# First-attention products issued one block later in a fused attention and quantised-layer kernel

## The chip, the cores and the metric

The kernel runs on one core of a Trainium2 chip. One launch computes all 16 images. The metric is the device time of that launch in microseconds. Six things work side by side on the core: TensorE (PE in the profile; its weight loads are PEld), VectorE (DVE), ScalarE (ACT), GpSimd (POOL), SyncE (SP, which here only issues transfers) and the DMA engines. Each engine runs its own list of instructions strictly in order and waits at semaphores for the others, so an instruction that waits holds everything behind it on its engine.

## The reference, cut to what matters

For each image, with x of 256 channels by 1024 places (tokens):

```python
def reference(x, norm_w, norm_b, qkv_w, qkv_b, proj_w, proj_b, ffn_w, ffn_b):
    xn = group_norm(x, norm_w, norm_b)                   # 8 groups
    q, k, v = split(einsum('oc,bchw->bohw', qkv_w, xn) + qkv_b)
    attn = softmax(einsum('bci,bcj->bij', q, k) / sqrt(C))
    x = x + (einsum('oc,bchw->bohw', proj_w, einsum('bij,bcj->bci', attn, v)) + proj_b)
    t = to_tokens(x)
    y = layer_norm(t)
    yn = y / (norm(y) + 1e-12)
    s = einsum('bid,bjd->bij', yn, yn)
    t = t + einsum('bij,bjd->bid', softmax(s * s), y)    # second attention
    z = layer_norm(t) @ (sign(w - mean(w)) * mean(abs(w))) + ffn_b
    t = t + round(clip(z, -1, 1) * 7) / 7
    return from_tokens(t)
```

## The kernel before

**Tiling.** The 1024 tokens are 8 blocks of 128. A 1024x1024 score matrix is made block by block: one block is 128 rows by 1024 columns. Every fp32 operand is kept as two rounded parts, a high one (`_hi`) and the rest (`_lo`), and each product is three matmuls (lo by hi, hi by lo, hi by hi).

**First attention, per block n.** TensorE makes `scores1(n)` in `wide[n % 2]` (L369). VectorE takes the row maximum, `row_max` (L989). ScalarE takes the exponential, `exp1` (L733). The block is then needed transposed. VectorE transposes inside 32x32 squares, `e1_turn` (L996); SyncE sends it to a scratch in HBM, `send` (L321), and fetches it back in the other order as four transfers, `fetch` (L328). ScalarE rounds it, `e1T_hi` (L740), VectorE takes the rest, `e1T_lo` (L1001), and only then can TensorE run `product1(n)` (L471 to L473, 24 matmuls). A product follows its block's scores by several blocks, to cover this round trip. `residual1(n)` on VectorE (L1010 to L1017) adds the input and takes the layer norm's statistics.

**After it.** For small groups of blocks (`GROUPS1`: two, two, two, one, one) GpSimd works out the layer norm's coefficients and lengths (L1250 to L1273), ScalarE makes `layer_norm1` (L750, L754) and `unit_rows` (L762), TensorE transposes these (`turn_cos`, L500), ScalarE and VectorE split them (`cosT_hi` L774, `cosT_lo` L1023). `scores2` (L369) makes the lower triangle of the symmetric second scores, `exp2` (L787, L789) their exponentials, and `turn_e2` (L530), `e2T_parts` (L1040, L1042) the upper triangle. `product2` follows in `back`.

**Between batches.** The older image `f = b - 1` runs its last layer inside `front(b, f)`: `turn_ln2`, `ffn`, and two output turns, `turn_t(f, 0)` and `turn_t(f, 1)` (L577), whose results VectorE adds in `output` (L1079). The next image's group norm statistics (`gn_sums` L952, L954) are taken on VectorE in the same stretch, and two tiny matmuls average them over groups, `group_means` (L411) and `group_vars` (L416).

**What sets the order.** The order of each engine's calls is written out by hand in the five functions `front`, one for each engine. There is no scheduler and no priority. The loop runs over images 1 to 14; image 0 and image 15 are written out with the same functions.

**Semaphores that matter below.** `scores1(n)` waits for `exp1(n - 2)`, since they share `wide[n % 2]`. `product1(n)` waits for `e1T_lo(n)`. `fetch(n)` waits for `send(n)` to have landed and for `e1T_lo(n - 2)`. `e1T_hi(n)` waits for `fetch(n)` and `product1(n - 2)`. `product1(4)` uses the bank that `output(f, 1)` must have read. `scores2(0)` waits for `cosT_lo(0)`. `scores2(4)` waits for `cosT_lo(2)`.

Of the kernel before, what the change touches and what calls it, by code (L numbers as in the profile page):

```python
# [45 lines left out]
def build(nc, x, norm_w, norm_b, qkv_w, qkv_b, proj_w, proj_b, ffn_w, ffn_b, out):  # L46
# [22 lines left out]
    with ExitStack() as ctx:  # L69
# [223 lines left out]
        def _(sp):  # L293
# [36 lines left out]
            def front(b, f):  # L330
# [8 lines left out]
                fetch(b, 3)  # L339
                fetch(b, 4)  # L340
                send(b, 5)
                fetch(b, 5)
                send(b, 6)
                fetch(b, 6)
                send(b, 7)
# [18 lines left out]
        def _(pe):  # L364
# [216 lines left out]
            def front(b, f, more):  # L581
# [37 lines left out]
                if f is not None:  # L619
                    pe.wait_ge(y_made, 4 * f + 4)  # L620
                    turn_t(f, 0)
                product1(b, 0)
                scores1(b, 5)
# [3 lines left out]
                product1(b, 1)  # L627
                scores1(b, 6)
                product1(b, 2)
                scores1(b, 7)  # L630
                turn_cos(b, 0)
                product1(b, 3)
# [7 lines left out]
                product1(b, 5)  # L640
                product1(b, 6)
                turn_cos(b, 1)
                turn_e2(b, 1)
                product1(b, 7)
                scores2(b, 2)
                turn_cos(b, 2)
                scores2(b, 3)
                turn_e2(b, 2)
                if more:
                    pe.wait_ge(t1_made, NT * b + 6)  # L650
                    group_means(b + 1)
# [3 lines left out]
                if more:  # L655
                    group_vars(b + 1)
# [3 lines left out]
                scores2(b, 6)  # L660
                turn_e2(b, 5)
# [42 lines left out]
        def _(act):  # L704
# [100 lines left out]
            def front(b, f, more, reuse=True):  # L805
# [20 lines left out]
                exp1(b, 4)  # L826
                e1T_hi(b, 2)
                exp1(b, 5)
                e1T_hi(b, 3)
                layer_norm1(b, 0)  # L830
                exp1(b, 6)
                unit_rows(b, 0)
                e1T_hi(b, 4)
                cosT_hi(b, 0)
                exp1(b, 7)
                e1T_hi(b, 5)
                e1T_hi(b, 6)
                exp2(b, 0)
                exp2(b, 1)
                layer_norm1(b, 1)  # L840
                unit_rows(b, 1)
                e1T_hi(b, 7)
                layer_norm1(b, 2)
                cosT_hi(b, 1)
                unit_rows(b, 2)
                layer_norm1(b, 3)
                exp2(b, 2)
                cosT_hi(b, 2)
# [3 lines left out]
                unit_rows(b, 4)  # L852
                cosT_hi(b, 3)
                exp2(b, 4)
                cosT_hi(b, 4)
# [42 lines left out]
        def _(dve):  # L898
# [183 lines left out]
            def front(b, f, more):  # L1082
# [29 lines left out]
                row_max(b, 4)  # L1112
                if f is not None:
                    output(f, 0)
                e1_turn(b, 4)
                e1T_lo(b, 1)
                residual1(b, 0)
                row_max(b, 5)
                e1T_lo(b, 2)
                e1_turn(b, 5)  # L1120
                residual1(b, 1)
                if f is not None:
                    output(f, 1)
                row_max(b, 6)
# [250 lines left out]
```

## Time and profile before

| | us |
|---|---|
| median of 3 runs | 1841.47 |
| lowest, highest | 1837.36, 1841.86 |
| the profiled execution | 1838.67 |
| its span in the profile | 1836.7 |
| TensorE busy | 1761.3 (96%) |
| VectorE busy | 1330.1 (72%) |
| ScalarE busy | 945.8 (51%) |
| GpSimd busy | 735.2 (40%) |
| HBM traffic | 92 GB/s over the span |

TensorE's busy time is a union of overlapping matmuls, so a busy TensorE still may be slowed by its clock. The idle time of the other engines costs nothing by itself. What counts are the places where TensorE waits, and these repeat nearly alike in each image. All rows from one image below are from batch 5, whose first attention runs around 600 to 645 us of the span.

### The profile page before, as it was taken

Reading aid. Unit: us, or ns where it says so; the run is one execution under the profiler, and the core shown is the slowest. Engines: PE = TensorE matmul, PEld = TensorE weight load, DVE = VectorE, ACT = ScalarE, POOL = GpSimd, SP = SyncE. Lnnn points to the kernel's source line nnn. Section 1 sums busy time; section 2 is a strip of 40 time slices with the busy share of each in tenths; the row PEclk is TensorE's granted clock in tenths of the full one; section 3 lists DMA queues with packets and bytes.
Section 4 is the critical chain, followed back from the end, with each engine's and each line's share of the span. In section 5 each row is a group of like instructions: output and inputs, shape, how many; then the busy total and the mean of one; then the engine's idle time right before and its main releaser. Section 6 shows DMA issues by size and latency. Waiting matters only on the chain.

```text
span 1836.7 us, 34581 instructions
## 1 busy us (share of the span) xinstructions
PE 1761.3 (96%) x11810; PEld 1610.9 (88%) x11810; DVE 1330.1 (72%) x2596; ACT 945.8 (51%) x1476; POOL 735.2 (40%) x1334
## 2 busy tenths in 40 slices
PE   8999999999999999999999999999999999999997
PEld 6898888988889888898988989888898888998887
DVE  6767767687676877768777686776868768686675
ACT  3645546455464554635456354564545545455462
POOL 0442615327162361624516245261542715326161
PEclk9999999999999999999999999999999999999998
DMA  3405124050330604216042150412405134050330
GB/s 122 140 24 155 52 95 133 23 174 32 118 111 33 193 2 133 96 40 189 0 148 80 57 171 14 158 57 74 154 23 164 42 99 129 23 178 28 95 113 24
DMA packets 108575, 169.67 MB, mean 92 GB/s; under 512 B 12928, under 2 KB 79872, under 8 KB 108544
## 3 DMA queue, kind: packets, MB, share of 16 engines
q1 hardware_dynamic: 108544, 169.27, 29.0%
q8 instruction: 18, 0.29, 0.1%
q14 instruction: 13, 0.11, 0.0%
HBM read 85.33 MB, written 83.89 MB: 92 GB/s over the span
## 4 chain that ended last, share of the span: by engine, by line
PE 55%; issue 19%; POOL 11%; DVE 8%; ACT 4%; DMA 1%; SPq 0%; POOLq 0%; DVEq 0%; ACTq 0%
PE wide L369 21%; PE narrow L369 5%; PE narrow L471 4%; PE narrow L473 4%; PE wide L471 4%; PE narrow L472 3%; PE wide L473 3%; PE wide L472 3%; PE turn L530 2%; DVE gn_stats L952 2%; POOL ln_r L1253 2%; PE turn L424 2%; PE turn L569 2%; PE turn L560 1%; POOL ln_shift L1255 1%
## 5 line engine op out<-in xcount | busy, mean ns | idle before, releaser
L369 PE MATMUL wide<-xn_hi,prob 128*128 128x512 f32 x1024 | 303.8, 398 | 0.3 <-ACT expo L733 0.3
L1250 POOL TENSOR_TENSOR ln_v<-ln_mv,ln_eps 128x2 f32<-128x2 f32 (+2 forms) x128 | 34.1, 266 | 542.3 <-DVE ln_mv L1017 332.9
L369 PEld LDWEIGHTS wide<-xn_hi,prob 128*128 128x128 f32 x1024 | 185.5, 188 | 39.2 <-ACT expo L733 0.7
L740 ACT ACTIVATE prob<-e_back 128x1024 fp32r<-128x1024 f32 x128 | 135.4, 1058 | 149.2 <-DMA e_back<-e_scratch 134.7
L767 ACT ACTIVATE ln<-tok,ln_shift,ln_r 128x256 f32<-128x256 f32 x128 | 68.5, 593 | 263.9 <-POOL ln_shift L1255 263.9
L996 DVE STREAM_TRANSPOSE x_norm<-expo 128x1024 f32<-128x1024 f32 x128 | 159.1, 1243 | 48.3 <-ACT expo L733 41.6
L733 ACT ACTIVATE expo<-wide,neg_max 128x1024 f32<-128x1024 f32 x128 | 142.3, 1111 | 98.9 <-DVE neg_max L989 98.9
L1001 DVE TENSOR_TENSOR prob<-e_back,prob 128x1024 fp32r<-128x1024 f32 x128 | 155.5, 1214 | 45.6 <-ACT prob L740 44.8
L989 DVE TENSOR_REDUCE neg_max<-wide 128x1 f32<-128x1024 f32 x128 | 155.2, 1212 | 41.4 <-PE wide L369 41.4
L1295 POOL TENSOR_TENSOR carrier_p<-ones 128x1 f32<-128x1 f32 x60 | 11.7, 195 | 415.4 <-DVE y_sb L1065 412.8
L369 PE MATMUL wide<-xn_lo,prob 128*128 128x512 f32 x512 | 160.7, 394 | 0.0
L1285 POOL TENSOR_TENSOR prob<-expo,prob 128x128 fp32r<-128x128 f32 (+6 forms) x112 | 143.1, 1290 | 36.8 <-DVE prob L1029 36.8
L471 PE MATMUL narrow<-prob 128*128 128x256 f32 x512 | 147.7, 288 | 1.9 <-DVE prob L1001 1.9
L471 PE MATMUL wide<-val,prob 128*128 128x258 f32 x512 | 147.1, 287 | 0.0
L471 PE MATMUL narrow<-val,prob 128*128 128x258 f32 x512 | 146.9, 287 | 0.0
L473 PE MATMUL narrow<-prob 128*128 128x256 f32 x512 | 145.4, 284 | 0.0
L472 PE MATMUL narrow<-prob 128*128 128x256 f32 x512 | 145.3, 284 | 0.0
L473 PE MATMUL wide<-val,prob 128*128 128x258 f32 x512 | 145.1, 283 | 0.0
L473 PE MATMUL narrow<-val,prob 128*128 128x258 f32 x512 | 145.1, 283 | 0.0
L472 PE MATMUL wide<-val,prob 128*128 128x256 f32 x512 | 144.6, 282 | 0.0
L472 PE MATMUL narrow<-val,prob 128*128 128x256 f32 x512 | 144.6, 282 | 0.0
L471 PE MATMUL wide<-prob 128*128 128x256 f32 x384 | 114.4, 298 | 23.4 <-DVE prob L1001 23.4
(182 smaller groups left out, 5466.8 us busy)
## 6 DMA issues: line engine op xcount, KB each, us to landing
e_scratch<-x_norm SPq DMA_DIRECT2D x128, 512.0 KB, 3.0
e_back<-e_scratch SPq DMA_DIRECT2D x512, 128.0 KB, 3.1
x_raw<-in_x SPq DMA_DIRECT2D x32, 512.0 KB, 4.0
out<-y_sb SPq DMA_DIRECT2D x32, 512.0 KB, 3.7
tok<-in_L_conv_qkv_w SPq DMA_DIRECT2D x1, 768.0 KB, 6.6
ln<-in_L_conv_proj_w SPq DMA_DIRECT2D x1, 256.0 KB, 6.8
ln<-in_L_ffn_weight SPq DMA_DIRECT2D x1, 256.0 KB, 3.9
out_bias<-in_L_conv_proj_b SPq DMA_DIRECT2D x1, 128.0 KB, 3.8
```

The costliest lines, as they stand in the source:

```text
L369: mm = pe.matmul(o, lhsT, r, start=first and i == 0, stop=last and i == len(parts) - 1)
L424: mm = pe.transpose(turn[:, t * C + k * P:t * C + (k + 1) * P], x_raw[:, k, tile(HT * g + t)], ident[:, :])
L471: pe.matmul(o[:, 0:w], hi, value_hi(j), start=j == 0, stop=False)
L472: pe.matmul(o[:, 0:C], hi, value_lo(j), start=False, stop=False, skip_group_check=True)
L473: mm = pe.matmul(o[:, 0:w], lo, value_hi(j), start=False, stop=j == NT - 1)
L733: act.activation(expo[:, n % DEEP], wide[n % 2][:, :], ACT.Exp, bias=neg_max[:, n:n + 1], accum_out=row_sum1[:, n:n + 1]).then_inc(e1_made, 1)
L740: act.activation(eT_hi[:, n % 2].rearrange("p (n i t) -> p n i t", n=NT, i=SQ), e_back[:, n % 2].rearrange("p i (n t) -> p n i t", n=NT), ...
L767: act.activation(ln2[:, n], tok[:, n], ACT.Identity, bias=ln2_shift[:, n:n + 1], scale=ln2_r[:, n:n + 1]).then_inc(ln2_made, 1)
L989: dve.tensor_reduce(neg_max[:, n:n + 1], wide[n % 2][:, :], AX.X, ALU.max, negate=True).then_inc(max_made, 1)
L996: dve.transpose(e_turned[:, n % 2].rearrange("p (q n t) -> p n q t", q=SQ, n=NT), expo[:, n % DEEP].rearrange("p (n q t) -> p n q t", q=SQ ...
L1001: dve.tensor_sub(eT_lo[:, n % 2].rearrange("p (n i t) -> p n i t", n=NT, i=SQ), e_back[:, n % 2].rearrange("p i (n t) -> p n i t", n=NT), ...
L1285: pool.tensor_sub(prob[:, 1, J, row], expo[:, J % DEEP, row], prob[:, 0, J, row].bitcast(F32)).then_inc(p_made, 1)
```

## The change

The calls in the five hand-written orders are moved; none is added or taken away, and no line of a called function changes.

- TensorE: `scores1(5)`, `scores1(6)` and `scores1(7)` each stand one place earlier against the products. `turn_t(f, 1)` stands after `scores1(7)` and no longer before `product1(1)`. `turn_cos(1)` and `turn_cos(2)` stand earlier, `group_means` and `group_vars` later.
- ScalarE: `exp1(5)`, `exp1(6)`, `exp1(7)` come earlier against the rounding `e1T_hi`; `layer_norm1(0)` comes after `exp1(7)`.
- VectorE: the row maxima, turns, rests and residuals are reordered to match. `output(f, 1)` comes after `row_max(7)`. `gn_sums(b + 1, 1)`, `gn_deviation` and `gn_variance` come later.
- SyncE: `send(5)`, `send(6)` and `send(7)` each stand one place ahead of a `fetch`.
- GpSimd's order is the same.

```diff
--- before.py
+++ after.py
@@ -337,12 +337,12 @@
                 fetch(b, 2)
                 send(b, 4)
                 fetch(b, 3)
+                send(b, 5)
                 fetch(b, 4)
-                send(b, 5)
+                send(b, 6)
                 fetch(b, 5)
-                send(b, 6)
+                send(b, 7)
                 fetch(b, 6)
-                send(b, 7)
                 fetch(b, 7)
                 if f is not None:
                     store(f, 0)
@@ -619,17 +619,17 @@
                 if f is not None:
                     pe.wait_ge(y_made, 4 * f + 4)
                     turn_t(f, 0)
+                scores1(b, 5)
                 product1(b, 0)
-                scores1(b, 5)
+                scores1(b, 6)
+                product1(b, 1)
+                scores1(b, 7)
                 if f is not None:
                     pe.wait_ge(out_made, 2 * f + 1)
                     turn_t(f, 1)
-                product1(b, 1)
-                scores1(b, 6)
                 product1(b, 2)
-                scores1(b, 7)
+                product1(b, 3)
                 turn_cos(b, 0)
-                product1(b, 3)
                 if f is not None:
                     pe.wait_ge(out_made, 2 * f + 2)
                 else:
@@ -638,26 +638,26 @@
                 scores2(b, 0)
                 scores2(b, 1)
                 product1(b, 5)
+                turn_cos(b, 1)
                 product1(b, 6)
-                turn_cos(b, 1)
                 turn_e2(b, 1)
                 product1(b, 7)
+                turn_cos(b, 2)
                 scores2(b, 2)
-                turn_cos(b, 2)
                 scores2(b, 3)
                 turn_e2(b, 2)
-                if more:
-                    pe.wait_ge(t1_made, NT * b + 6)
-                    group_means(b + 1)
                 scores2(b, 4)
                 turn_cos(b, 3)
                 turn_e2(b, 3)
                 if more:
-                    group_vars(b + 1)
+                    pe.wait_ge(t1_made, NT * b + 6)
+                    group_means(b + 1)
                 scores2(b, 5)
                 turn_e2(b, 4)
                 turn_cos(b, 4)
                 scores2(b, 6)
+                if more:
+                    group_vars(b + 1)
                 turn_e2(b, 5)
                 scores2(b, 7)
                 scores2(b, 8)
@@ -824,34 +824,34 @@
                     ffn_out(f, 1, reuse)
                 e1T_hi(b, 1)
                 exp1(b, 4)
+                exp1(b, 5)
                 e1T_hi(b, 2)
-                exp1(b, 5)
+                exp1(b, 6)
                 e1T_hi(b, 3)
+                exp1(b, 7)
                 layer_norm1(b, 0)
-                exp1(b, 6)
+                e1T_hi(b, 4)
                 unit_rows(b, 0)
-                e1T_hi(b, 4)
+                e1T_hi(b, 5)
                 cosT_hi(b, 0)
-                exp1(b, 7)
-                e1T_hi(b, 5)
+                layer_norm1(b, 1)
                 e1T_hi(b, 6)
+                unit_rows(b, 1)
                 exp2(b, 0)
                 exp2(b, 1)
-                layer_norm1(b, 1)
-                unit_rows(b, 1)
+                cosT_hi(b, 1)
                 e1T_hi(b, 7)
                 layer_norm1(b, 2)
-                cosT_hi(b, 1)
                 unit_rows(b, 2)
                 layer_norm1(b, 3)
+                cosT_hi(b, 2)
                 exp2(b, 2)
-                cosT_hi(b, 2)
                 unit_rows(b, 3)
                 exp2(b, 3)
                 layer_norm1(b, 4)
-                unit_rows(b, 4)
                 cosT_hi(b, 3)
                 exp2(b, 4)
+                unit_rows(b, 4)
                 cosT_hi(b, 4)
                 exp2(b, 5)
                 exp2(b, 6)
@@ -1110,55 +1110,55 @@
                 if f is not None:
                     clip(f, 1)
                 row_max(b, 4)
+                e1T_lo(b, 1)
+                e1_turn(b, 4)
                 if f is not None:
                     output(f, 0)
-                e1_turn(b, 4)
-                e1T_lo(b, 1)
+                row_max(b, 5)
+                e1_turn(b, 5)
                 residual1(b, 0)
-                row_max(b, 5)
+                row_max(b, 6)
                 e1T_lo(b, 2)
-                e1_turn(b, 5)
+                e1_turn(b, 6)
                 residual1(b, 1)
+                e1T_lo(b, 3)
+                row_max(b, 7)
                 if f is not None:
                     output(f, 1)
-                row_max(b, 6)
-                e1T_lo(b, 3)
-                e1_turn(b, 6)
-                row_max(b, 7)
+                e1_turn(b, 7)
+                residual1(b, 2)
                 e1T_lo(b, 4)
-                e1_turn(b, 7)
+                residual1(b, 3)
+                e1T_lo(b, 5)
                 cosT_lo(b, 0)
-                e1T_lo(b, 5)
-                residual1(b, 2)
-                residual1(b, 3)
+                residual1(b, 4)
                 e1T_lo(b, 6)
-                residual1(b, 4)
                 e2_hi(b, 0)
                 e2_hi(b, 1)
                 residual1(b, 5)
+                cosT_lo(b, 1)
                 e1T_lo(b, 7)
                 residual1(b, 6)
-                cosT_lo(b, 1)
+                e2T_parts(b, 1)
                 if more:
                     gn_sums(b + 1, 0)
-                e2T_parts(b, 1)
                 residual1(b, 7)
+                cosT_lo(b, 2)
+                e2_hi(b, 2)
+                e2T_parts(b, 2)
+                e2_hi(b, 3)
                 if more:
                     gn_sums(b + 1, 1)
-                e2_hi(b, 2)
-                cosT_lo(b, 2)
-                e2T_parts(b, 2)
-                if more:
-                    gn_deviation(b + 1)
-                e2_hi(b, 3)
                 cosT_lo(b, 3)
                 e2T_parts(b, 3)
                 if more:
-                    gn_variance(b + 1)
+                    gn_deviation(b + 1)
                 e2_hi(b, 4)
                 e2T_parts(b, 4)
                 cosT_lo(b, 4)
                 e2_hi(b, 5)
+                if more:
+                    gn_variance(b + 1)
                 e2T_parts(b, 5)
                 e2_hi(b, 6)
                 e2_hi(b, 7)
```

On ScalarE, in the loop's `front`, this stands before, from `exp1(6)` (its source is `wide0`) over `unit_rows(0)`, `e1T_hi(4)`, `cosT_hi(0)` and `exp1(7)` (`wide1`) to `e1T_hi(5)` and `e1T_hi(6)`:

```order
L733 ACTIVATE expo,row_sum1<-wide0,neg_max 128x1024
L758 REGISTER_ALU
L762 ACTIVATE cos_x<-ln_x,len_i 128x256 x2
L737 REGISTER_ALU
L740 ACTIVATE prob<-e_back 128x1024
L774 ACTIVATE tokT_hi<-narrow1 128x2x256
L730 REGISTER_ALU
L733 ACTIVATE expo,row_sum1<-wide1,neg_max 128x1024
L740 ACTIVATE prob<-e_back 128x1024
L737 REGISTER_ALU
L740 ACTIVATE prob<-e_back 128x1024
```

and now, from `exp1(6)` over `e1T_hi(3)`, `exp1(7)`, `layer_norm1(0)` (L750, L754), `e1T_hi(4)` and `unit_rows(0)` to `e1T_hi(5)`:

```order
L733 ACTIVATE expo,row_sum1<-wide0,neg_max 128x1024
L740 ACTIVATE prob<-e_back 128x1024
L730 REGISTER_ALU
L733 ACTIVATE expo,row_sum1<-wide1,neg_max 128x1024
L746 ISA
L750 ACTIVATE ln_x<-tok,ln_shift,ln_r 128x256 x2
L754 ACTIVATE val<-ln_x 128x2x256
L737 REGISTER_ALU
L740 ACTIVATE prob<-e_back 128x1024
L758 REGISTER_ALU
L762 ACTIVATE cos_x<-ln_x,len_i 128x256 x2
L740 ACTIVATE prob<-e_back 128x1024
```

The first layer norm, the rounding of block 4 and the first unit rows stood ahead of block 7's exponential and stand behind it now.

On VectorE, at the last row maximum (its source is `wide1`), this stands before, from `output(f, 1)` over `row_max(6)`, `e1T_lo(3)`, `e1_turn(6)`, `row_max(7)`, `e1T_lo(4)` and `e1_turn(7)` to `cosT_lo(0)`:

```order
L1079 TENSOR_TENSOR y_sb<-turn,y_sb 128x1024
L988 REGISTER_ALU
L989 TENSOR_REDUCE neg_max<-wide0 128x1
L1001 TENSOR_TENSOR prob<-e_back,prob 128x1024
L995 REGISTER_ALU
L996 STREAM_TRANSPOSE x_norm<-expo 128x8x4x32
L988 REGISTER_ALU
L989 TENSOR_REDUCE neg_max<-wide1 128x1
L1001 TENSOR_TENSOR prob<-e_back,prob 128x1024
L996 STREAM_TRANSPOSE x_norm<-expo 128x8x4x32
L1022 ISA
L1023 TENSOR_TENSOR tokT_lo<-narrow1,tokT_hi 128x2x256
```

and now, from `e1T_lo(3)` over `row_max(7)`, `output(f, 1)`, `e1_turn(7)` and `residual1(2)` to `e1T_lo(4)`:

```order
L1001 TENSOR_TENSOR prob<-e_back,prob 128x1024
L988 REGISTER_ALU
L989 TENSOR_REDUCE neg_max<-wide1 128x1
L1079 TENSOR_TENSOR y_sb<-turn,y_sb 128x1024
L996 STREAM_TRANSPOSE x_norm<-expo 128x8x4x32
L1010 RECIPROCAL inv_sum1<-row_sum1 128x1
L1012 SCALAR_TENSOR_TENSOR tok<-narrow0,inv_sum1,x_tok 128x256
L1015 BN_STATS ln_stats<-tok 128x6
L902 MEMSET carrier 128x1
L1017 BN_AGGR ln_mv<-ln_stats 128x2
L1001 TENSOR_TENSOR prob<-e_back,prob 128x1024
```

The output of the older image moved behind the last row maximum, and the rest of block 4 moved behind the last turn and a residual.

On VectorE, after `residual1(7)`, this stands before, from `gn_sums(b + 1, 1)` to `cosT_lo(2)`:

```order
L952 BN_STATS gn_stats<-x_raw 128x6 x2
L901 REGISTER_ALU
L902 MEMSET carrier 128x1
L954 BN_AGGR gn_mv<-gn_stats 128x2
L1028 REGISTER_ALU
L1029 CAST prob<-expo 128x384
L1022 REGISTER_ALU
L1023 TENSOR_TENSOR tokT_lo<-narrow1,tokT_hi 128x2x256
```

and now, from `cosT_lo(2)` over `e2_hi(2)`, `e2T_parts(2)` and `e2_hi(3)` to the same group norm sums:

```order
L1023 TENSOR_TENSOR tokT_lo<-narrow1,tokT_hi 128x2x256
L1028 REGISTER_ALU
L1029 CAST prob<-expo 128x384
L1039 REGISTER_ALU
L1040 CAST prob<-turn 128x2x128
L1042 TENSOR_TENSOR prob<-turn,prob 128x2x128
L1028 REGISTER_ALU
L1029 CAST prob<-expo 128x512
L952 BN_STATS gn_stats<-x_raw 128x6 x2
L901 REGISTER_ALU
L902 MEMSET carrier 128x1
L954 BN_AGGR gn_mv<-gn_stats 128x2
```

The sums moved from ahead of `cosT_lo(2)` to behind block 3's copy.

## Rows read from the trace of the kernel before

**Rows 1.** Waits of TensorE: engine, line, releaser: us in total, times, longest

```profile
PE wide L471 <- DVE prob L1001: 23.4, 16, 1.7
PE narrow L411 <- DVE gn_mv L954: 15.8, 13, 7.3
PE narrow L500 <- ACT cos_x L762: 11.5, 16, 0.9
PE wide L369 <- DVE tokT_lo L1023: 7.7, 16, 0.6
```

**Rows 2.** TensorE in order of time, batch 5: start us, duration us, engine, line, operation

```profile
610.00 1.06 PE L577 MATMUL turn<-ident,tok 128*128 128x128 f32 x8
...
613.77 0.64 PE L369 MATMUL wide<-xn_hi,prob 128*128 128x512 f32 x2
...
616.57 1.03 PE L577 MATMUL turn<-ident,tok 128*128 128x128 f32 x8
```

**Rows 3.** TensorE, the same view, later in batch 5; idle time before a row in brackets

```profile
632.10 0.28 PE L471 MATMUL turn<-prob 128*128 128x256 f32 x1
...
634.98 0.22 PE L369 MATMUL wide<-tokT_hi,tokT_lo 128*128 128x128 f32 x1
...
636.37 0.28 PE L471 MATMUL narrow<-prob 128*128 128x256 f32 x1
...
643.06 0.63 PE L500 MATMUL narrow<-ident,cos_x 128*128 128x128 f32 x4 [0.78 <-ACT cos_x L762]
...
645.25 0.39 PE L471 MATMUL wide<-prob 128*128 128x256 f32 x1 [1.45 <-DVE prob L1001]
...
653.81 0.56 PE L369 MATMUL wide<-tokT_hi,tokT_lo 128*128 128x384 f32 x2 [0.48 <-DVE tokT_lo L1023]
...
656.37 0.59 PE L369 MATMUL wide<-tokT_hi,tokT_lo 128*128 128x512 f32 x2
```

**Rows 4.** VectorE in order of time, same batch

```profile
610.56 1.22 DVE L989 TENSOR_REDUCE neg_max<-wide 128x1 f32<-128x1024 f32 x1
...
616.52 0.15 DVE L1010 RECIPROCAL inv_sum<-row_sum 128x1 f32<-128x1 f32 x1
...
617.79 1.23 DVE L989 TENSOR_REDUCE neg_max<-wide 128x1 f32<-128x1024 f32 x1
...
629.00 1.22 DVE L989 TENSOR_REDUCE neg_max<-wide 128x1 f32<-128x1024 f32 x1 [0.60 <-PE wide L369]
...
643.97 1.23 DVE L1001 TENSOR_TENSOR prob<-e_back,prob 128x1024 fp32r<-128x1024 f32 x1 [2.59 <-ACT prob L740]
```

**Rows 5.** ScalarE in order of time, same batch

```profile
611.97 1.06 ACT L740 ACTIVATE prob<-e_back 128x1024 fp32r<-128x1024 f32 x1 [2.05 <-DMA e_back<-e_scratch]
...
624.17 1.10 ACT L750 ACTIVATE ln_x<-tok,ln_shift,ln_r 128x256 f32<-128x256 f32 x2 [1.43 <-POOL ln_shift L1255]
...
625.84 1.10 ACT L733 ACTIVATE expo<-wide,neg_max 128x1024 f32<-128x1024 f32 x1
...
628.12 1.04 ACT L740 ACTIVATE prob<-e_back 128x1024 fp32r<-128x1024 f32 x1
```

**Rows 6.** GpSimd in order of time, same batch

```profile
637.36 1.17 POOL L1250 TENSOR_TENSOR ln_v<-ln_mv,ln_eps 128x2 f32<-128x2 f32 x1 [8.91 <-DVE ln_mv L1017]
```

**Rows 7.** SyncE queue in order of time, same batch

```profile
637.15 1.73 SPq L328 DMA_DIRECT2D e_back<-e_scratch  x4
```

**Rows 8.** DMA issues: bytes of one, median us from issue to landing

```profile
e_back<-e_scratch SPq DMA_DIRECT2D x512, 128.0 KB, 3.1
```

**Rows 9.** Two neighbouring batches: us, TensorE busy (instructions), granted clock, DMA share, GB/s

```profile
529.55:643.06 113.51, 109.81 (x736) 0.98 0.28 92
643.06:754.95 111.89, 108.25 (x737) 1.00 0.29 93
```

**Rows 10.** 3.4 us before and after a fall of the granted clock, same columns

```profile
536.20:539.60 3.40, 2.40 (x14) 1.00 0.00 0
539.60:543.00 3.40, 2.91 (x13) 0.66 0.00 0
```

## The prediction

> **What bounds the kernel now.** I read the share of busy time first, then the waits of TensorE, then one batch in order of time on every engine. TensorE is busy for 96% of the span, so the change can only touch its waits and its clock. Four waits matter [rows 1]: the first attention's last product waits for its rest (23.4 us over 16 batches), `group_means` waits for the group sums (15.8, of which 7.3 are one wait at the start), `turn_cos(1)` waits for the unit rows (11.5), and `scores2(4)` waits for `cosT_lo(2)` (7.7). Without the 7.3 that is 51 us, 3.2 in a batch. These waits stand late in the first attention and after it: 0.78 us ahead of 643.06, 1.45 ahead of 645.25, 0.48 ahead of 653.81 [rows 3]. No product before the last one waits for its rest. The reader is to see that the other engines bound the tail of a stage whose body TensorE bounds.
>
> A second cost is TensorE's clock. Neighbouring batches take 113.51 and 111.89 us, with a mean granted clock of 0.98 and 1.00 [rows 9]. In the slower one the clock fell from 2.4 to 1.2 GHz for some 3 us, right behind the stretch with the short waits: 2.40 of 3.40 us busy ahead, then a mean clock of 0.66 [rows 10]. One fall costs about 1.6 us, and one batch in two has it.
>
> **TensorE's side of the change.** An output turn and the product behind it take 613.77 - 610.00 = 3.77 us together, a score block 616.57 - 613.77 = 2.80 [rows 2], a product alone 634.98 - 632.10 = 2.88 [rows 3]; so the turn is some 0.8, its product starting a little slower. I follow batch 5. Everything up to the output turn at 610.00 is unchanged. The new order gives `scores1(5)` 610.8 to 613.6, `product1(0)` to 616.5, `scores1(6)` to 619.3, `product1(1)` to 622.2, `scores1(7)` to 625.0. One output turn and one product have moved from ahead of the last score block to behind it, so it ends 3.8 us earlier than the 628.8 that the old order gives (616.57 + 0.8 + 2.9 + 2.8 + 2.9 + 2.8). TensorE does the same work, so this is worth nothing unless the last product's rest comes as much earlier.
>
> **VectorE's side.** Its large instructions let the next one start after 1.14 us (a duration of 1.22 less an overlap of 0.08), a residual after 617.79 - 616.52 = 1.27 [rows 4]. ScalarE's exponential takes 1.2 us with its sum. From `row_max(4)` at 610.56 the new order is:
> - `e1T_lo(1)` has to wait for its rounding, which ends at 611.97 + 1.06 = 613.03 [rows 5]. The old order had `output(f, 0)` in this hole. So `e1T_lo(1)` 613.1, `e1_turn(4)` 614.3, `output(f, 0)` 615.4, `row_max(5)` 616.6 to 617.8. The old order had it at 617.79 [rows 4].
> - `exp1(5)` to 619.0, `e1_turn(5)` 619.1, `residual1(0)` 620.2, `row_max(6)` 621.5, `e1T_lo(2)` 622.7, `e1_turn(6)` 624.0, `residual1(1)` 625.2, `e1T_lo(3)` 626.5, `row_max(7)` 627.6.
>
> The old order had `row_max(7)` at 629.00 [rows 4]. So of the 3.8 us only 1.4 arrive: VectorE's queue is the limit, not the scores.
>
> **ScalarE's side, where the change costs.** `exp1(7)` runs 628.9 to 630.0. `layer_norm1(0)` stands behind it, although its coefficients are there by then; its three instructions take 625.84 - 624.17 = 1.67 us [rows 5]. `e1T_hi(4)` comes next, 631.7 to 632.7, where the old order had it at 628.12 [rows 5], ahead of `exp1(7)`. Then `e1T_lo(4)` ends at 634.0 and `product1(4)` starts at 634.05. The old start was 632.10 [rows 3]. TensorE meanwhile has done `turn_t(f, 1)`, `product1(2)` and `product1(3)` by 625.0 + 0.8 + 2.9 + 2.9 = 631.6. **A new wait of 2.1 us** stands here, part of it written down to `turn_cos(0)`, whose unit rows come at 633.5.
>
> **What it gives back.** `product1(4)` to 637.0, two small score blocks 636.37 - 634.98 = 1.4 [rows 3] to 638.4, `product1(5)` to 641.3. The statistics of `residual1(3)` are there at 635.3. In the old trace GpSimd started on that group at 637.36 and the turn on TensorE at 643.06, 5.7 us later [rows 3, 6]; this now gives 641.0, so the wait of 0.8 ahead of `turn_cos(1)` goes. `product1(6)` runs 641.8 to 644.7. `e1T_hi(7)` stands behind the two first `exp2` and `cosT_hi(1)` and ends at 643.9. VectorE has `residual1(5)` and `cosT_lo(1)` ahead of `e1T_lo(7)`, which then runs 644.6 to 645.8 (old: 643.97 [rows 4]). The last product starts at 645.85, against 645.25 [rows 3]. Its wait shrinks from 1.45 to about 1.0.
>
> **Behind it.** `turn_cos(2)` now stands right behind the last product, and its unit rows are some 0.3 us late. `turn_e2(2)` waits for `exp2(2)`, some 0.6 us, as ScalarE has `layer_norm1(3)` ahead. The wait of 0.48 ahead of `scores2(4)` goes, since the group sums no longer stand ahead of `cosT_lo(2)`. They stand behind the copy of block 3 now and end at 656.3, so `group_means` waits 0.7 us as before. `scores2(5)` starts at 656.5, against 656.37 [rows 3], and `group_vars` (0.14 us) no longer is ahead of it. **Sum: 0.3 us a batch more, 5 us in 16 batches.** Later steps (`product2`, the older image's layer) have the same order and start from there; image 0 has no older image and is counted like the rest.
>
> **Transfers.** `fetch(4)` now waits for `e1T_lo(2)`, which ends at 623.9. Landing takes 1.73 of issue and up to 3.1 more [rows 7, 8], so 628.7 at the latest; `e1T_hi(4)` takes it at 631.7. Cover 3 us. `fetch(7)` follows `e1T_lo(5)`, 636.5, lands by 641.3, and is taken at 642.8. Cover 1.5 us. The sends gain a place and lose nothing. I take 0 for all of these; if the covers went, each us late is paid once.
>
> **How far off the sum can be.** The step with the widest play is GpSimd's first instruction of a group. Started during a VectorE instruction with two inputs in SBUF, it took 1.17 us [rows 6], and I assumed that again; without it `e1T_lo(6)`, the last product and the second coefficient chain come up to 0.9 earlier, of which TensorE could use some 0.5. The other end is two such hits more, and the slower first matmul after each wait, together 0.8 a batch. So the sum lies between -0.2 and +1.1 us a batch, -3 to +18 in all. I take +0.3, since the rows that it hangs on show the hit.
>
> **The clock.** Nothing in the trace says when it will fall with the waits elsewhere. The bounds are no fall (8 x 1.6 = 13 us gained) and one in each batch (13 lost). I take a fall or two less, -2 us, as the longest single stretch of waits before (0.78 and 1.45 close together) is broken up. The Trainium skill, "TensorE: Matmul & The Clock Gate", section "Why this matters for your kernels", warns only of idle gaps longer than any that stand here. By that rule the clock would have stayed up, and the new wait would cost no more than its length, 1841.5 + 5 = 1846.5. The trace disagrees already: the clock fell behind waits of at most 1.45 us [rows 3, 10].
>
> **Rivals.**
> - **A, balance (0.41).** As worked out: +5 for the waits and -2 for the clock, so 1838.7 + 3 = 1841.7 for the profiled execution. The median of three stands 2.8 us over that execution, so 1844.5. Its own range is 1837 to 1847.
> - **B, faster (0.24).** The last product's rest comes early enough, because GpSimd is not held up, and the falls of the clock behind it go. -3 for the waits and -8 for five falls less: 1841.5 - 11 = 1830.5. For it: the old waits stand exactly where the clock fell. Against: VectorE hands on only 1.4 of the 3.8 us.
> - **C, slower (0.24).** The new wait of 2.1 us ahead of `product1(4)` is the longest of all. If the clock falls behind it in each batch, 8 falls come on top: 1841.5 + 5 + 13 = 1859.5. It decides once the wait there is about as long as the two old ones together (2.2 us, and 2.1 is forecast); `layer_norm1(0)` behind `exp1(7)` is its cause. Against: the old pair of waits brought a fall in one batch of two only.
> - **D, slower by the later chain (0.11).** Coefficients of the third and fourth group, each late by the hit on GpSimd: 0.8 a batch more than A, 1841.5 + 13 + 3 = 1857.
>
> That the change does not do what it says is no rival here: the order is what is written, and no planner stands between.
>
> **How the numbers follow.** The forecast is A, 1844.5 us. B lies below the bound of 0.3% (5.5 us, about what a measurement of this kernel can tell from no change), C and D above it. So faster 0.24, same 0.41, slower 0.35. The range that leaves out two in ten, one at each end, is 1830 to 1860; it takes in -3 to +18 for the waits.
>
> **What would show it.** In the new profile: TensorE waits about 2 us ahead of `product1(4)` (line L471 into `turn`) or `turn_cos(0)`, in each batch; the wait ahead of the last product is near 1.0; the one of `scores2(4)` for `cosT_lo` is gone, that of `group_means` stays. `row_max(7)` comes about 17.0 us after `row_max(4)`. If the wait ahead of `product1(4)` is under 1 us, the reading of ScalarE's queue is wrong and B is right. If the waits sum as said and the time does not, it is the clock.

## The result and the profile after

The changed kernel takes 1835.8 us (median of 20), the kernel before 1840.2 us (median of 20). The ratio is 0.9978, with a 95% interval of 0.9970 to 0.9985. That is 0.22% faster: inside the band of 0.3% that the prediction called the same, but clear of zero and on the other side of the forecast, which stood 0.16% above the median of before that it knew. The profiled execution takes 1835.49 us.

The span and the first part of the page of the changed kernel, beside the table of before:

```profile
span 1833.8 us, 34581 instructions
...
PE 1753.4 (96%) x11810; PEld 1603.2 (87%) x11810; DVE 1370.1 (75%) x2596; ACT 930.8 (51%) x1476; POOL 726.8 (40%) x1334
```

TensorE's waits in the changed kernel (same columns as [rows 1]):

```profile
PE narrow L500 <- ACT cos_x L762: 32.8, 32, 2.3
PE narrow L411 <- DVE gn_mv L954: 17.9, 16, 7.3
PE turn L530 <- ACT expo L789: 10.1, 16, 0.7
PE wide L471 <- DVE prob L1001: 6.0, 9, 0.7
```

Two of the four of before have shrunk or gone: the last product waited 23.4 us in all and waits 6.0, and `scores2(4)` no longer waits for `cosT_lo(2)`. New is a wait for the unit rows ahead of `turn_cos(0)` (nearly all of the 32.8), and the one for `exp2(2)` has grown to 10.1. Without the one at the start (7.3) the four add up to 59.5 us, against 51 of the four in [rows 1]. The wait for `exp2(2)` was 3.3 us before and is not in that 51:

```profile
PE turn L530 <- ACT expo L789: 3.3, 12, 0.3
```

So some 5 us of waits have come. **By its waits the kernel should be slower.**

Batch 5 on TensorE, the places of [rows 3]. The first output turn, at 610.00 in before, starts at 608.96 here, so 1.04 us is to be added to these times to set them beside the prediction's:

```profile
632.64 0.63 PE L500 MATMUL narrow<-ident,cos_x 128*128 128x128 f32 x4 [1.84 <-ACT cos_x L762]
633.15 0.39 PE L471 MATMUL turn<-prob 128*128 128x256 f32 x1
...
644.76 0.39 PE L471 MATMUL wide<-prob 128*128 128x256 f32 x1 [0.68 <-DVE prob L1001]
...
648.09 0.63 PE L500 MATMUL narrow<-ident,cos_x 128*128 128x128 f32 x4 [0.20 <-ACT cos_x L762]
...
651.78 0.44 PE L530 MATMUL turn<-ident,expo 128*128 128x128 f32 x2 [0.63 <-ACT expo L789]
...
655.23 0.38 PE L411 MATMUL narrow<-gn_mv,group_mean 128*128 128x2 f32 x2 [0.70 <-DVE gn_mv L954]
655.48 0.59 PE L369 MATMUL wide<-tokT_hi,tokT_lo 128*128 128x512 f32 x2
```

VectorE (`row_max(4)`, `row_max(7)`, `e1T_lo(4)`, `cosT_lo(2)`) and ScalarE (`exp1(7)`, `layer_norm1(0)` in two rows, `e1T_hi(4)`), the places of [rows 4] and [rows 5]:

```profile
609.51 1.22 DVE L989 TENSOR_REDUCE neg_max<-wide 128x1 f32<-128x1024 f32 x1
...
626.64 1.22 DVE L989 TENSOR_REDUCE neg_max<-wide 128x1 f32<-128x1024 f32 x1
...
631.80 1.30 DVE L1001 TENSOR_TENSOR prob<-e_back,prob 128x1024 fp32r<-128x1024 f32 x1 [0.17 <-ACT prob L740]
...
650.83 0.69 DVE L1023 TENSOR_TENSOR tokT_lo<-narrow,tokT_hi 128x512 fp32r<-128x512 f32 x1 [1.54 <-ACT tokT_hi L774]
```

```profile
627.90 1.11 ACT L733 ACTIVATE expo<-wide,neg_max 128x1024 f32<-128x1024 f32 x1 [3.95 <-DVE neg_max L989]
...
629.00 1.08 ACT L750 ACTIVATE ln_x<-tok,ln_shift,ln_r 128x256 f32<-128x256 f32 x2
630.12 0.63 ACT L754 ACTIVATE val<-ln_x 128x512 fp32r<-128x512 f32 x1
630.66 1.04 ACT L740 ACTIVATE prob<-e_back 128x1024 fp32r<-128x1024 f32 x1
```

GpSimd, the first coefficient instruction of the second group, as in [rows 6]:

```profile
634.45 1.09 POOL L1250 TENSOR_TENSOR ln_v<-ln_mv,ln_eps 128x2 f32<-128x2 f32 x1 [2.43 <-DVE ln_mv L1017]
```

Two neighbouring batches (columns of [rows 9]), from one start of `turn_cos(0)` to the next:

```profile
519.74:632.64 112.90, 109.54 (x737) 0.98 0.29 93
632.64:744.98 112.34, 108.30 (x736) 1.00 0.30 93
```

And the wait of `turn_cos(0)` with what follows it, in a batch with a fall of the clock and in the next one; then the wait alone and the time behind it alone, in the batch with the fall:

```profile
517.90:521.30 3.40, 1.56 (x8) 0.79 0.39 157
630.80:634.20 3.40, 1.56 (x12) 1.00 0.38 154
```

```profile
517.90:519.70 1.80, 0.00 (x0) 1.00 0.71 291
519.90:522.90 3.00, 3.00 (x16) 0.50 0.43 129
```

An undisturbed batch takes 112.34 us, 0.45 more than the 111.89 of before. A batch with a fall takes 112.90, where before it took 113.51 [rows 9]. Before, this fall cost 1.6 us; here it costs 0.56. The clock falls at 519.87, right behind the wait, while `turn_cos(0)` runs. Its slow product 4 makes TensorE busy for 1.24 us more (109.54 against 108.30) and eats the wait that the last product would have had (0.68 in an undisturbed batch, none in the other).

The clock record of the two traces has 14 falls before and 9 after; without the two at the very end, in both, 12 and 7. **What a fall costs depends on the waits that follow it:**

| falls in the trace | right behind | batch with one | costs |
|---|---|---|---|
| before, batches 1, 4, 6, 8, 10, 12, 14 | the waits of `turn_e2(2)`, `group_means`, `scores2(4)` (0.3, 0.7, 0.5) | 113.29 to 113.57 | 1.6 |
| before, batches 2 and 13 | the wait of the last product (1.45) | 111.90 and 111.88 | 0 |
| changed, batches 2, 4, 6, 8, 9, 11, 13 | the wait of `turn_cos(0)` (1.84) | 112.84 to 112.93 | 0.56 |

The other three of before lie in batch 0 (two) and in batch 15. The batch that costs nothing, in before:

```profile
1544.50:1656.38 111.88, 109.22 (x736) 0.98 0.29 93
```

TensorE is busy for 0.98 us more there (109.22 against 108.25), and the waits of `turn_e2(2)` and `group_means` behind the fall, 0.98 us together, are gone. So in batches 1 to 14 the change did not lower the number of falls that cost something, seven and seven, but their price.

In the profiled pair the thirteen batches from the second on take the same time, 112.64 us each (before, then changed):

```profile
192.07:1656.38 1464.31, 1418.58 (x9568) 0.99 0.29 93
182.03:1646.45 1464.42, 1416.66 (x9569) 0.99 0.30 93
```

A longer undisturbed batch and cheaper falls cancel there. By the starts of `turn_cos(4)` the changed kernel is 1.9 us ahead in batch 1 and still 1.9 us ahead in batch 14. The rest of the 2.9 us between the two spans comes behind it.

### The profile page after: what moved, and what is told of

Read it like the earlier page. It is cut to its first block, busy times and chain, and to the rows that moved or that the text cites. A ratio compares the mean times of both kernels' runs of the same rounds, so it can differ in the third digit from the quotient of the medians.

```text
span 1833.8 us, 34581 instructions
## 1 busy us (share of the span) xinstructions
PE 1753.4 (96%) x11810; PEld 1603.2 (87%) x11810; DVE 1370.1 (75%) x2596; ACT 930.8 (51%) x1476; POOL 726.8 (40%) x1334
## 4 chain that ended last, share of the span: by engine, by line
PE 52%; issue 19%; POOL 15%; ACT 6%; DVE 6%; DMA 1%; POOLq 1%; SPq 0%; ACTq 0%; DVEq 0%
PE wide L369 19%; PE narrow L369 5%; PE narrow L471 4%; PE narrow L473 3%; PE wide L471 3%; PE narrow L472 3%; PE wide L473 3%; PE wide L472 3%; POOL ln_r L1253 2%; PE turn L530 2%; POOL ln_v L1250 2%; POOL val L1279 2%; POOL sq_root L1267 2%; PE turn L424 2%; PE turn L569 2%
## 5 line engine op out<-in xcount | busy, mean ns | idle before, releaser
L1250 POOL TENSOR_TENSOR ln_v<-ln_mv,ln_eps 128x2 f32<-128x2 f32 (+2 forms) x128 | 55.3, 432 | 508.7 <-DVE ln_mv L1017 300.6
L369 PE MATMUL wide<-tokT_hi,tokT_lo 128*128 128x512 f32 (+3 forms) x384 | 122.9, 361 | 0.0
```

The costliest lines, as they stand in the source:

```text
L369: mm = pe.matmul(o, lhsT, r, start=first and i == 0, stop=last and i == len(parts) - 1)
L1250: pool.tensor_add(v[:, cols], mv[:, cols, 1], ln_eps[:, one]).then_inc(steps, 1)
```

## The experiments

Two theories stand. **Clock:** the order itself is slower, as forecast, and the gain is that the falls of the clock cost less. **Waits:** the late waits that went are the gain, and the clock falls as it likes. All times are medians; ratios are to the kernel before, run on the same chip in the same rounds.

### Activity in the waits of the kernel before

```diff
+            def fill(o, count):
+                for _ in range(count):
+                    pe.matmul(o, sign_w[:, 0, 0:P], sign_w[:, 0, :], start=True, stop=True)
...
+                fill(out1[7][:, 0:C], 6)
                 turn_cos(b, 1)
                 turn_e2(b, 1)
+                fill(out1[7][:, 0:C], 11)
                 product1(b, 7)
...
+                    fill(narrow[0][:, 0:C], 5)
                     group_means(b + 1)
...
+                if J == 4:
+                    pe.wait_ge(sq2_made, NP * b + J - 1)
+                    fill(wide[0][:, 0:C], 3)
```

> The kernel before, with 25 extra small matmuls of constants in each batch, into banks that the next instruction overwrites, placed inside TensorE's four waits (6 ahead of turn_cos(1), 11 ahead of the last product, 5 ahead of group_means, 3 ahead of scores2(4); about 0.12 us each). The waits last as long as before, only TensorE is active in them. Clock theory (the gain of the change is fewer falls of the clock, and these follow inactive stretches): the falls go, 12 of them at 1.2 to 1.6 us, so 1840 minus 12 to 18, about 1825 us, and the granted clock is near 1.0 throughout. Rival (the waits themselves are what the change saves, and the clock falls for other reasons): same time as before or slightly more, 1840 to 1844 us, with as many falls.

Measured: 1827.8 us, ratio 0.9930 (0.9916 to 0.9945). Its waits, and one batch:

```profile
PE narrow L411 <- DVE gn_mv L964: 7.3, 1, 7.3
PE turn L537 <- ACT expo L799: 4.2, 15, 0.4
```

```profile
539.66:651.56 111.90, 111.32 (x762) 1.00 0.29 94
```

The waits are now filled, the batch is 111.90 us long as the undisturbed one of before was, and its clock is 1.00. The trace has 3 falls for 14, one in batch 0 and two at the end. More work, 11 us less time: the falls of the clock were caused by TensorE's short inactivity, and they cost the kernel before some 11 us (10.9 by the medians; by the ratio 13, 10 to 15). Seven falls at 1.6 us, as the trace has them, are 11.2.

### The same in the changed kernel

```diff
                     pe.wait_ge(t1_made, NT * b + 2)
+                    fill(narrow[1][:, 0:C], 14)
                 pe.wait_ge(cos_made, NT * b + n1)
```

> The changed kernel, with 14 extra small matmuls of constants in each batch inside the new wait ahead of turn_cos(0), where all seven falls of its clock lie. Clock theory: the falls go, at some 0.6 us each, so 4 us less, about 1832 us. Rival: no change, 1836 us, or more if the extra matmuls delay something.

Measured: 1833.8 us, ratio 0.9966 (0.9953 to 0.9978). Two neighbouring batches are alike now:

```profile
531.39:643.78 112.39, 110.05 (x751) 1.00 0.29 93
```

Only the two falls at the end are left, and 2.0 us are saved; I had expected 4, from 0.6 us each. With the clock out of the way the two orders can be compared: 1833.8 - 1827.8 = **6.0 us slower** for the changed order, 112.39 against 111.90 in a batch. The forecast for the waits was +5. Falls cost 10.9 us in the order before (1838.7 in these rounds less 1827.8) and 2.0 in the changed one (1835.8 less 1833.8), so the clock's part of the change is -8.9. The two parts make -2.9 where the result has -4.3, since the median of the kernel before was 1840.2 in the rounds of the result and 1838.7 in these: the split is good to 1 or 2 us, its signs are not in doubt.

### Work added where TensorE never waits

```diff
                     return prob[:, 0, j, tile(n)], prob[:, 1, j, tile(n)]
 
+                if n == 5:
+                    fill(out2[1][:, 0:C], 4)
```

> The kernel before with 4 extra small matmuls (0.48 us of TensorE work) in each batch ahead of product2(5), where TensorE never waits. Plain sum: 16 batches times 0.48 = 8 us slower, 1848 us. Clock theory: the undisturbed batch grows from 111.9 to 112.4 us, as in the changed kernel, and falls become rarer, one in more than two batches, which gives back most of it: 1840 to 1843 us.

> The kernel before with 8 extra small matmuls (0.96 us) a batch ahead of product2(5). Plain sum: 15 us slower than before, 1855 us. Clock theory: the undisturbed batch is 112.9 us, above the mean of 112.65 at which the falls came out before, so most falls are gone (14 became 13 with half the work added); what is not given back is at most 15 less 12 falls at 1.3, so 1842 to 1848 us.

Measured with 4: 1841.2 us, ratio 1.0007 (0.9997 to 1.0016), so by the ratio 1.3 us (at most 3) for 8 us of added work. With 8: 1842.9 us, ratio 1.0029 (1.0019 to 1.0040), so 5 us for 15. Two batches of the first:

```profile
529.09:641.32 112.23, 108.68 (x740) 1.00 0.29 92
641.32:755.12 113.80, 110.20 (x740) 0.99 0.29 92
```

The added work is there, as the undisturbed batch is 112.23 us and the other 113.80. The falls are 13 with four and 11 with eight extra matmuls, but most of them stand in the place where they are free. One such batch, with a fall behind the last product's wait:

```profile
1206.04:1318.40 112.36, 109.71 (x741) 0.98 0.29 93
```

Of the falls in batches 1 to 14, seven stood in the dear place before, two do with four extra matmuls (batches 5 and 9) and one with eight (batch 1, 113.95 us). At 1.6 us each that gives back 8 and 10 us. The undisturbed batch is longer by 0.42 and by 0.96 us, 7 and 15 us in all. The sums are -1 and +5; the profiled executions stand 0.8 below and 3.5 above the one of before. Why the falls moved is not shown.

### The group part alone, the products' part alone

The first has the kernel before with the later `group_means`, `group_vars`, `gn_sums`, `gn_deviation` and `gn_variance`:

```diff
-                if more:
-                    pe.wait_ge(t1_made, NT * b + 6)
-                    group_means(b + 1)
                 scores2(b, 4)
                 turn_cos(b, 3)
                 turn_e2(b, 3)
                 if more:
-                    group_vars(b + 1)
+                    pe.wait_ge(t1_made, NT * b + 6)
+                    group_means(b + 1)
                 scores2(b, 5)
```

> The kernel before with only the later place of group_means, group_vars and the group sums; products, scores and output turns as before. By the sums of waits: the wait ahead of scores2(4) (0.48) goes, the one ahead of group_means stays near 0.7, so 0.3 to 0.6 us a batch less on an undisturbed batch, 5 to 8 us. Rival, that the clock holds the batch at the same mean: 1838 to 1841 us, the shorter batch paid with more falls.

Measured: 1839.1 us, ratio 0.9995 (0.9986 to 1.0004). The 5 to 8 us that I expected are not there. The time is the rival's, but its reason, a shorter batch paid for with more falls, is not what happened:

```profile
PE wide L471 <- DVE prob L1001: 23.8, 17, 1.7
PE wide L369 <- DVE tokT_lo L1023: 20.0, 16, 1.5
PE narrow L411 <- DVE gn_mv L954: 7.3, 1, 7.3
```

The wait of `group_means` has gone (7.3 is the one at the start), and the one of `scores2(4)` has grown from 7.7 to 20.0, as TensorE gets there earlier and `cosT_lo(2)` does not. The undisturbed batch is longer, some 112.2 us against 111.9, and the falls are fewer, 12 for 14.

The second is the changed kernel with the group part as before:

```diff
                 turn_e2(b, 2)
+                if more:
+                    pe.wait_ge(t1_made, NT * b + 6)
+                    group_means(b + 1)
                 scores2(b, 4)
                 turn_cos(b, 3)
                 turn_e2(b, 3)
                 if more:
-                    pe.wait_ge(t1_made, NT * b + 6)
-                    group_means(b + 1)
+                    group_vars(b + 1)
                 scores2(b, 5)
```

> The changed kernel with group_means, group_vars and the group sums where they stood before; scores, products and output turns as changed. Waits as I read them now: ahead of turn_cos(0) 1.84 us as in the changed kernel; ahead of scores2(4) about 0.5 again, since the sums again stand ahead of cosT_lo(2). So up to 0.5 us a batch above the changed kernel, 8 us. Clock theory: part of that is given back, 1836 to 1842 us. Rival (the later groups are the whole gain): 1840 us or more, with the clock falling as often as before (14 times).

Measured: **1828.6 us**, ratio 0.9937 (0.9925 to 0.9950), 7 us faster than the whole change. My expectation was 1836 to 1842.

```profile
PE narrow L500 <- ACT cos_x L762: 31.8, 32, 1.9
PE turn L530 <- ACT expo L789: 10.0, 16, 0.7
PE narrow L411 <- DVE gn_mv L954: 7.3, 1, 7.3
PE wide L471 <- DVE prob L1001: 4.7, 7, 0.7
```

```profile
519.08:631.25 112.17, 109.54 (x737) 0.98 0.29 94
631.25:742.85 111.60, 108.19 (x736) 1.00 0.30 94
```

The wait of `group_means` has gone and none has come for `cosT_lo(2)`. The profile of the changed kernel has the reason, in its row of VectorE at 650.83: it is idle for 1.54 us ahead of `cosT_lo(2)`, whose rounding is late. In the old place the group sums fill this hole for nothing. In the new place they stand behind block 3's copy and `group_means` waits 0.70 us for them, 15 times. The falls are nearly as many as before (12 for 14) but cheap: 112.17 us against 111.60.

With 14 fills inside the wait of `turn_cos(0)` in this kernel:

> The products-only kernel with 14 extra small matmuls of constants inside the wait of turn_cos(0). All ten of its falls in batches lie in that wait and cost 0.5 us each. Clock theory: no falls in the batches, 1828.6 less 5, about 1823 us; that is 16 times 0.3 us under the filled kernel before (1827.8), the sum of the waits alone. Rival (falls cost nothing here): 1828 us.

Measured: 1821.4 us, ratio 0.9904 (0.9889 to 0.9919). The trace has 3 falls, so nine have gone and with them 7 us, 0.8 each. And the products' part alone is 6.4 us faster than before when neither has falls in its batches (1827.8 - 1821.4), which is 0.4 us a batch. The +6.0 us of the whole change are thus -6.4 for the products and +12.4 (1833.8 - 1821.4) for the later group sums and means on top of them. The falls of this kernel do not lie in the wait, as the expectation has it, but 0.4 to 1.6 us behind its end.

### The queue of ScalarE behind the new wait

```diff
                 exp1(b, 7)
-                layer_norm1(b, 0)
                 e1T_hi(b, 4)
+                layer_norm1(b, 0)
                 unit_rows(b, 0)
...
                 e1_turn(b, 7)
-                residual1(b, 2)
                 e1T_lo(b, 4)
+                residual1(b, 2)
...
                 product1(b, 3)
-                turn_cos(b, 0)
...
                 product1(b, 4)
+                turn_cos(b, 0)
+                product1(b, 5)
                 scores2(b, 0)
                 scores2(b, 1)
-                product1(b, 5)
```

> The changed kernel with three further moves: on ScalarE e1T_hi(4) ahead of layer_norm1(0), on VectorE e1T_lo(4) ahead of residual1(2), on TensorE turn_cos(0) behind product1(4) and the two first blocks of the second scores behind product1(5). If the new wait of 1.84 us is the place of e1T_hi(4) behind the layer norm, as the prediction said, product1(4) starts some 1.6 us later than product1(3) ends no more but about 0.8 us; shorter by 0.3 to 1.0 us a batch, 1820 to 1832 us with the clock's part. Rival (VectorE's or the transfers' pace holds block 4): the wait moves to product1(4) with its old length, 1836 us or more.

Measured: 1827.7 us, ratio 0.9930 (0.9917 to 0.9943). TensorE in batch 5:

```profile
627.99 0.39 PE L471 MATMUL turn<-prob 128*128 128x256 f32 x1 [0.76 <-DVE prob L1001]
...
631.72 0.36 PE L471 MATMUL narrow<-prob 128*128 128x256 f32 x1 [0.16 <-DVE prob L1001]
...
636.39 0.63 PE L500 MATMUL narrow<-ident,cos_x 128*128 128x128 f32 x4 [0.17 <-ACT cos_x L762]
...
640.86 0.39 PE L471 MATMUL wide<-prob 128*128 128x256 f32 x1 [0.79 <-DVE prob L1001]
...
651.33 0.38 PE L411 MATMUL narrow<-gn_mv,group_mean 128*128 128x2 f32 x2 [0.71 <-DVE gn_mv L954]
```

The wait of 1.84 has become 0.76 ahead of `product1(4)`, 0.16 ahead of `product1(5)` and 0.17 ahead of `turn_cos(1)`. That the new wait comes from the place of `e1T_hi(4)` behind the layer norm, as the prediction said, fits this, and the rows of the changed kernel have the chain: `e1T_hi(4)` follows the layer norm at 630.66, VectorE stands idle for it and ends the rest at 633.10, `product1(4)` starts at 633.15. The three moves were measured together only, so their shares are not shown.

No fall is left in the batches, although nothing was filled. With 0.19 ahead of `turn_cos(2)` and 0.63 ahead of `turn_e2(2)` TensorE waits 3.4 us in this batch, and 3.7 in an undisturbed one of before. None of the waits here is above 0.8 us, and they stand over 3 us apart; those of before stood in two groups, two and three of them close together. The sum of the waits alone does not bring the falls.

The other swap was on the kernel before, and took away what ended its longest wait:

```diff
                 layer_norm1(b, 1)
-                unit_rows(b, 1)
                 e1T_hi(b, 7)
+                unit_rows(b, 1)
```

> The kernel before with one swap on ScalarE: e1T_hi(7) ahead of unit_rows(1). If the last product's wait is ScalarE's queue, as the trace has it (the rounding begins at 642.82, the block's data is there near 641.5), the wait of 1.45 us goes down to about 0.3 and the one of turn_cos(1) grows from 0.78 to about 1.2: 1.0 us a batch less, 1823 to 1830 us. Rival by the clock: the shorter batch is paid back with more falls, 1836 to 1840 us.

> The kernel before with that swap and with extra small matmuls of constants inside the waits (9 ahead of turn_cos(1), 3 ahead of the last product, 5 ahead of group_means, 3 ahead of scores2(4)). Clock theory: with no falls left the whole saving of the swap arrives, 1.0 us a batch under the filled kernel's 1828: about 1812 us. Rival (the swap saves nothing on TensorE's path): 1828 us.

Measured: 1838.2 us, ratio 0.9991 (0.9981 to 1.0001), and with fills (9 and 3 in place of 6 and 11 at the two waits that moved) 1829.0 us, ratio 0.9936 (0.9922 to 0.9950), where 1827.8 was the filled kernel without the swap. The gain that I expected is not there:

```profile
642.54 0.63 PE L500 MATMUL narrow<-ident,cos_x 128*128 128x128 f32 x4 [1.44 <-ACT cos_x L762]
...
647.22 0.44 PE L369 MATMUL wide<-tokT_hi,tokT_lo 128*128 128x384 f32 x1 [1.06 <-DVE tokT_lo L1023]
```

`turn_cos(1)` waits 1.44 us in place of 0.78. The last product no longer waits, but `scores2(2)` behind it does, 1.06 us, for `cosT_lo(1)`: `unit_rows(1)`, now later, is the start of that chain. The wait has moved one call on and to `turn_cos(1)`, and the filled pair shows that this is not the clock's doing.

### Both finds together

The changed kernel with the three moves of block 4 and with the group part as before:

> Both finds together: block 4 rounded ahead of the layer norm as in the kernel with the shorter new wait (1827.7 us), and the group sums, group_means and group_vars where they stood before. The wait of 0.70 ahead of group_means goes as it did in the products-only kernel, 16 times 0.7 = 10 us if no falls come: about 1817 us. Rival (the two savings share one slack, or falls come back): 1824 to 1828 us.

Measured: **1814.6 us**, ratio 0.9872 (0.9857 to 0.9887), faster than both kernels (1.3% under before, 1.2% under the change).

```profile
PE wide L471 <- DVE prob L1001: 12.4, 16, 0.8
PE turn L471 <- DVE prob L1001: 11.4, 15, 0.8
PE turn L530 <- ACT expo L789: 10.1, 16, 0.7
PE narrow L500 <- ACT cos_x L762: 5.8, 32, 0.2
```

It is 13 us below the kernel with the three moves alone, where 10 were expected. Its waits are spread out, none above 0.83 us in batches 1 to 15, and the clock stays up in all batches but the first.

## Why the prediction was wrong

**The waits were right in size.** With the shift of 1.04 us between the two traces:

| step | forecast | measured + 1.04 |
|---|---|---|
| `row_max(7)` | 627.6 | 627.68 |
| `e1T_hi(4)` starts | 631.7 | 631.70 |
| wait ahead of `turn_cos(0)`, `product1(4)` | 2.1 | 1.84 |
| `product1(4)` starts | 634.05 | 634.19 |
| last product starts | 645.85 | 645.80 |
| wait ahead of it | 1.0 | 0.68 |
| waits of `turn_cos(2)`, `turn_e2(2)`, `group_means` | 0.3, 0.6, 0.7 | 0.20, 0.63, 0.70 |
| `scores2(5)` starts | 656.5 | 656.52 |

That VectorE's queue hands on only 1.4 of the 3.8 us, that ScalarE's order makes the new wait, and that `scores2(4)` stops waiting all came so. `turn_cos(1)` does not wait, as was said. A batch is 0.45 us longer (0.3 forecast), and the whole 6.0 us with the clock out of play (5 forecast). One reason was wrong. The wait ahead of `scores2(4)` was to go because the group sums no longer stand ahead of `cosT_lo(2)`; in the products-only kernel they stand there and the wait is gone all the same. So the later place of the sums, taken as a small gain, costs 12.4 us on top of the products, and the earlier products, taken as a loss, gain 6.4.

**The clock's term failed.** The step was: "I take a fall or two less, -2 us". It measured -8.9 us (10.9 of falls before, 2.0 after), more than the +6.0 of the waits. The prediction had named this sign itself: if the waits sum as said and the time does not, it is the clock. Two things were wrong in the term.
- I priced a fall at 1.6 us wherever it stands. In the changed kernel it stands ahead of another wait and costs 0.56 by the two batches, less in the medians. My count of dear falls, one batch in two, was about right: seven in the trace, and 7 x 1.6 = 11.2 is what the filled kernel gave back. Five more were there, of which the two in batches 2 and 13 are free; what those in batches 0 and 15 cost is not shown.
- I took the waits of 0.78 and 1.45 as what brings the falls. The dear ones, the one of [rows 10] among them, stand behind the next group, `turn_e2(2)`, `group_means` and `scores2(4)` (0.3, 0.7, 0.5). That group the change breaks up, and no fall stands behind it any more.

The absolute forecast was also 1.3 us high from the start, as the median of three that it stood on (1841.5) was above the one of twenty (1840.2). That 1835.8 lies within 1830 to 1860 says little for the working: the range is wide.

Rival B had the sign, faster through the clock, but for the wrong waits: it asked that GpSimd not hold up the chain, and GpSimd was held up (1.09 us in the row at 634.45). Rival C's wait was there, and falls moved behind it, all seven; but they came in place of the old ones, in seven batches of sixteen, and were cheap. The rule of the Trainium skill ("TensorE: Matmul & The Clock Gate", section "Why this matters for your kernels"), which warns of longer idle gaps only, is contradicted by the filled kernel before: activity in waits of at most 1.7 us took 11 falls away, seven of which stood behind waits of at most 0.7 us.

What stays open is why the falls come in the batches where they do, and why they take the one place or the other. No run shows it.

## What to carry to other kernels

When TensorE bounds a kernel and its clock still falls in a few places, price the falls first: fill the waits with harmless matmuls and take the time again. That gives the cost of the waits and of the clock apart, and here the two had opposite signs. Do not count falls, but look at what a fall costs: one with waits behind it may be free, one in busy work is not. A wait that ends in another queue moves on when it is taken away alone (`unit_rows(1)`), and a filler in a hole is free only as long as it stays in that hole (the group sums): look for the idle time ahead of the next instruction on that engine before moving one away.

## What the runs showed of the hardware

- TensorE's granted clock falls from 2.4 to 1.2 GHz behind short waits: three of 0.3, 0.7 and 0.5 us or two of 0.8 and 1.45 us close together before, a single one of 1.84 us in the changed kernel. It stays up when these are filled with small matmuls: 3 falls against 14, and 2 against 9.
- A fall of some 3 us costs 1.6 us where TensorE is busy from then on, 0.56 us where a wait of 0.68 follows, and nothing where waits of 0.28 and 0.70 follow.
- Added TensorE work is not paid in full: 8 us of it cost 1.3 us, 15 us cost 5 us. In the traces of these runs most falls stand in a place where they cost nothing.
